# Feed-forward of an attention + top-4-block layer: from all tokens with a mask to 80 pages of gathered rows

## What is computed

```
x = x + attn(cond(x, itok_B_0_7, L0_cond_weights), Wq, bq, Wk, bk, Wv, bv, Wo)
x = x + ffn(cond2(x, itok_B_1_198, L0_cond2_weights), Wr, br, W1, W2)
```

```
prob = softmax(xf @ Wr.T + br)            # 2048 tokens, 16 blocks
_, idx = top_k(prob, 4)                   # each token keeps 4 blocks
h = einsum('nf,ibf->nib', xf, W1b)        # block i: 128 hidden units
h = gelu(h) * mask[:, :, None]            # exact gelu
y = einsum('nib,fib->nf', h, W2b)
```

## Time and profile before

| | |
|---|---|
| median of 3 runs | 896.96 us (895.66 to 899.36) |
| profiled execution, span | 899.2 us |
| what lies around the span in its own run | not given apart; the slowest of the three runs, 899.36 us, is 0.2 above the span |
| PE / DVE / ACT / POOL busy | 96% / 49% / 41% / 11% |
| chain that ended last | PE 72%, DVE 10%, ACT 6%, DMA 5%, issue 4% |
| DMA | 71.52 MB in 99,746 packets, mean 80 GB/s |
| granted TensorE clock | mean 0.992 |

### The profile page before, as it was taken

How to read it: one execution, slowest core, us unless ns; L and a number is a source line. 1 busy time by engine, 2 the same in 40 slices (tenths; PEclk the granted TensorE clock), 3 DMA queues, 4 the chain that set the end, 5 groups by cost and what they waited for, 6 DMA issues and landing times.

```text
span 899.2 us, 14422 instructions
## 1 busy us (share of the span) xinstructions
PE 866.4 (96%) x5250; PEld 430.9 (48%) x5250; DVE 439.4 (49%) x829; ACT 371.4 (41%) x639; POOL 100.9 (11%) x104
## 2 busy tenths in 40 slices
PE   6999999999899999999999999999999999999998
PEld 3444554445454445544445544454445444544443
DVE  3779773248762248752268766542254125403510
ACT  4678642147632157531267535530253025203400
POOL 3311111102111002220001100110011001100000
PEclk8999999999999999999999999999999999999999
DMA  7632432013441013330124598104210321031001
GB/s 220 226 129 61 84 70 71 12 62 56 90 82 36 13 61 85 75 76 23 59 74 96 114 262 274 26 2 142 73 26 12 141 61 26 23 129 36 0 24 47
DMA packets 99746, 71.52 MB, mean 80 GB/s; under 512 B 75828, under 2 KB 75892, under 8 KB 99700
## 3 DMA queue, kind: packets, MB, share of 16 engines
q10 hardware_dynamic: 75056, 34.71, 16.4%
q1 hardware_dynamic: 24644, 36.20, 12.6%
HBM read 45.66 MB, written 8.45 MB: 60 GB/s over the span
## 4 chain that ended last, share of the span: by engine, by line
PE 72%; DVE 10%; ACT 6%; DMA 5%; issue 4%; ACTq 2%; SPq 0%; POOL 0%; DVEq 0%
PE Q L935 57%; PE F L935 12%; DMA mids<-att 4%; PE M L935 3%; ACT u L437 2%; DVE sq L719 2%; ACTq L458 2%; ACT sq L443 2%; DVE att L740 1%; DVE att L732 1%; DVE e L714 1%; PE Q L1109 1%; DMA cw<-in_cw_dram 1%; DVE wa L890 1%; ACT e L436 1%
## 5 line engine op out<-in xcount | busy, mean ns | idle before, releaser
L935 PE MATMUL Q<-hT,wa 128*128 128x512 f16 x1536 | 342.7, 381 | 1.8 <-ACT e L591 1.8
L935 PEld LDWEIGHTS Q<-hT,wa 128*128 128x128 f16 x1536 | 148.6, 98 | 173.5 <-issue 2.8
L935 PE MATMUL Q<-wb,mids 128*128 128x512 f16 x768 | 175.5, 380 | 2.0 <-DVE xres L747 1.9
L935 PE MATMUL Q<-kv,mids 128*128 128x512 f16 x512 | 154.9, 379 | 0.0
L935 PEld LDWEIGHTS Q<-wb,mids 128*128 128x128 f16 x768 | 71.6, 98 | 83.9 <-DVE xres L747 2.0
L591 ACT ACTIVATE e<-Q,zero 128x512 f32<-128x512 f32 x64 | 43.9, 687 | 137.2 <-PE Q L935 137.2
L935 PE MATMUL Q<-sq,mids 128*128 128x512 f16 x256 | 97.0, 379 | 0.0
L343 POOL TENSOR_TENSOR xs<-xin,xs 128x512 f16<-128x512 f32 x32 | 39.7, 1239 | 503.0 <-ACT cws L396 503.0
L747 DVE SCALAR_TENSOR_TENSOR xres<-Q,xres 128x512 f32<-128x512 f32 x32 | 22.0, 689 | 127.5 <-PE Q L935 127.5
L935 PEld LDWEIGHTS Q<-kv,mids 128*128 128x128 f16 x512 | 50.1, 98 | 59.1
L714 DVE SCALAR_TENSOR_TENSOR e<-e,u 128x512 f32<-128x512 f32 x64 | 46.4, 725 | 54.8 <-ACT u L437 54.7
(11 more groups left out here) (97 smaller groups left out, 743.8 us busy)
## 6 DMA issues: line engine op xcount, KB each, us to landing
xin<-in_x_dram SPq DMA_DIRECT2D x16, 256.0 KB, 3.0
mids<-in_wq_dram SPq DMA_DIRECT2D x4, 1024.0 KB, 8.5
mids<-in_wo_dram SPq DMA_DIRECT2D x4, 1024.0 KB, 5.3
xres<-in_x_dram SPq DMA_DIRECT2D x16, 256.0 KB, 2.7
x_dram<-xres SPq DMA_DIRECT2D x16, 256.0 KB, 2.1
xin<-x_dram SPq DMA_DIRECT2D x16, 256.0 KB, 2.7
wk<-mask_dram ACTq DMA_DIRECT2D x8, 512.0 KB, 5.3
wv<-mask_dram ACTq DMA_DIRECT2D x8, 512.0 KB, 7.2
```

The source lines that it names most:

```text
L935: last = nc.tensor.matmul(out, lhs(a), rhs(b), start=(k == 0 and q == 0), stop=(k == n - 1 and q == len(PASSES) - 1))
```

## The change

The feed-forward no longer runs all blocks for all tokens. For each pair of batches m (16 in all, `NT`) the conditioned tokens are split into float16 high and low parts and routed as before (`cond2`, `router`, `route`). Then two small matmuls count: a strictly triangular and an all-ones matrix times the 0/1 mask give each token's position within its block and the number of tokens per block (`count`). `position` on DVE keeps for each of the 16 blocks a current page of 128 rows; when it is full the block takes the next free page. The result is a row number for each of a token's 4 kept blocks (`slot`). The two float16 parts of the tokens are turned back to rows of 2 KB by a transposing DMA (`turn_rows`, ACT), and POOL writes each row to its 4 places in a DRAM buffer of 80 pages (`scatter`, four indirect DMAs of 128 rows). The buffer is filled with zeros first (10 stores of 2 MB, issued by SP in group 0). A table gives each page's block (`table`).

After the attention SP loads each page with a transposing DMA (`load_slots`), PE applies the 128 hidden units of that page's block (12 matmuls of 128 columns, weights addressed by a register that is loaded from the table), four pages share a PSUM bank, ACT makes gelu, and the second layer is 3 matmuls of 512 columns per page; y rows are stored to DRAM (`store_slots`). When all are stored, POOL gathers for each pair of batches 4 x 128 rows of 2 KB, DVE adds them and x1, and SP stores the result. All loops are written out instead of looped. The routing of groups 0 and 1 is placed in the attention of groups 2 and 3's preparation (`routing`, in the code the bodies g = 1 and 2), that of groups 2 and 3 in `last_body`. Mask, mask broadcast and `body_b` are gone.

```diff
+NT = NG * NP
+NS = 80
+NQ = NS // 4
+ROWS = NS * 128
+NX, NC = 8, 6
+FILL = 10
...
+            def fill(i):
+                r = NS // FILL
+                sp.dma_start(xg_d.rearrange("(p r) c -> p r c", p=128)[:, r * i:r * i + r, :],
+                             rows[:, 0, :].unsqueeze(1).to_broadcast([128, r, 2 * T])).then_inc(filled, 16)
...
+            def load_slots(t):
+                if t == 0:
+                    sp.wait_ge(o_free, NP * NG + 1)
+                    for q in scat:
+                        sp.wait_ge(q, 64 * NT // 2)
+                elif t >= NX:
+                    sp.wait_ge(w1_done, (t - NX) // 4 + 1)
+                sp.dma_start_transpose(xT[:, t % NX, :, :], xg_d[128 * t:128 * t + 128, :]).then_inc(x_ld[t % NX], 16)
...
+            for t in range(NX):
+                load_slots(t)
+            for q in range(NQ):
+                for t in range(4 * q + NX, min(4 * q + NX + 4, NS)):
+                    load_slots(t)
+                for t in range(4 * q, 4 * q + 4):
+                    store_slots(t)
...
+            def scatter(m):
+                s = m % 2
+                pool.wait_ge(placed, m + 1)
+                pool.wait_ge(rows_in[s], 16 * (m // 2 + 1))
+                for k in range(TOPK):
+                    pool.indirect_dma_start(xg_d, bass.IndirectOffsetOnAxis(ap=slot[:, m, k:k + 1], axis=0),
+                                            rows[:, s, :], None).then_inc(scat[s], 16)
...
+                    kv_split(g + 1, 1)
+                    x_split(1, g - 1, 0)
+                    x_split(1, g - 1, 1)
+                    x_split(1, g - 1, 2)
+                    scatter(m)
+                    kv_split(g + 1, 2)
+                    x_split(1, g - 1, 3)
+                    scatter(m + 1)
+                    kv_split(g + 1, 3)
...
+            for j in range(4):
+                pool.wait_ge(y_st[j], 16 * NQ)
+            for m in range(NT):
+                c = m % NC
+                if m >= NC:
+                    pool.wait_ge(out_st[c], 16 * (m // NC))
+                for k in range(TOPK):
+                    pool.indirect_dma_start(cb[c][:, k, :], None, y_d,
+                                            bass.IndirectOffsetOnAxis(ap=slot[:, m, k:k + 1], axis=0)).then_inc(got[c], 16)
...
+            def first_layer(q):
+                s = q % 2
...
+                for j in range(4):
+                    t = 4 * q + j
+                    expert[t] = t if t < NB else pe.value_load(tab[0:1, t:t + 1], min_val=0, max_val=NB - 1)
+                    pe.wait_ge(x_ld[t % NX], 16 * (t // NX + 1))
+                    for k in range(KC):
+                        last = product(Q[s][:, j * 128:(j + 1) * 128], lambda a: wa[:, a, k, bass.ds(expert[t] * 128, 128)],
+                                       lambda b: xT[:, t % NX, 4 * b + k, :], k, KC)
+                last.then_inc(w1_done, 1)
...
+            for q in range(1, NQ):
+                first_layer(q)
+                second_layer(q - 1)
```

1275 lines of the change are left out of this document (838 added, 437 removed).

## The result

The changed kernel takes 942.52 us (median of 4 runs, 941.06 to 946.44), the kernel before on the same chip 896.31 (895.38 to 899.36): ratio 1.052, 95% interval 1.049 to 1.055. It is 5% slower. The prediction was 886 us with a range up to 938 and "faster" as its likeliest sign: wrong in value, range and sign.

The account below looks back on a forecast made before the run. The prediction took TensorE's matmul columns to bound the feed-forward half. Its terms, 624 us to the end of attention and routing, 7 hand-over, 170 pages and 87 gathers, gave 888 us, less 2: 886 us, range 846 to 938.

Parts of the forecast that it names:

- (a): Attention groups 0 to 2: routing adds 16 us, with a 4 us stall per group; the page fill in group 0 adds nothing.
- if that cover goes: Page fill in group 0: x loads and turned tiles would land late and PE wait; no size given.
- (b): Last attention group: DVE becomes the bound with 68 us against PE's 31, plus 6 us for the last two m.
- (c): Hand-over to the pages: last four scatters at 1.25 us, 5 us, and a landing 2.0; SP starts at 631.
- (d): Pages: transfers are the bound at 8.2 us per four pages, PE's sequencer at 6.5 hidden; 170 us in all.
- (e): Gather and sum at the end: 64 gathers at 1.25 us on POOL, DVE's 42 us of additions hidden; 87 us.
- Rival 2: Scatters and gathers bare on the path: POOL's issue at 2.0 us each costs 51 us more, 937 us; chance 0.20.
- Rival 3: Pages: TensorE's clock falls to 0.50, four pages take 10.2 us, 926 us in all; chance 0.08.
- Rival 4: Groups 1 and 2: routing chain stalls PE 14 us per group instead of 4, 906 us; chance 0.05.
- The sign: Whole kernel against the one before: faster 0.61, same 0.07, slower 0.32.

Follow-up runs that it names:

- fill_few: Against the changed kernel, only the 30 pages left partly empty are filled with zeros, in 5 stores of 1.5 MB; 931.55 us, ratio 1.036 to the kernel before.
- fill_fine2: Against the changed kernel, zero fill in 40 paced 0.5 MB pieces, group 0's x loads and stores moved ahead, 16 pieces at the end; 939.27 us.
- late: Against the changed kernel, last residual addition moved earlier, 32 of 46 PE fillers removed, fill paced in 33 pieces in group 0 and 7 in group 1; 929.05 us.
- no_position: Changed kernel without `position`: constant slots and one small DVE copy per m in its place, output not the reference's; 925.28 us.
- plain: Changed kernel with pages loaded plainly instead of turned, same bytes, output not the reference's; 930.2 us, ratio 1.035 to the kernel before.
- static: Changed kernel with constants for the pages' block numbers, so no value loads or register addresses on PE there; 939.5 us, ratio 1.045 to the kernel before.
- few_adds: Changed kernel with the three additions per m in the tail cut to one of 8 columns; 934.74 us, ratio 1.043 to the kernel before.
- warm: Changed kernel with two filler matmuls on PE ahead of the wait of each page from 8 on; 947.6 us, ratio 1.054 to the kernel before.
- no_scatter: Changed kernel without the 64 scatters, so the pages stay zero and the output is not the reference's; 923.45 us.
- half_gather: Changed kernel with each gather fetching half a row, 1 KB instead of 2, at the same number of instructions; 938.38 us, ratio 1.047 to the kernel before.

## Why the prediction was wrong

- **(a), "there is room for it, so nothing": failed, 15 us.** The fill was priced by its share of the engines over 160 us. What counts is who is behind a burst: two stores of 2 MB hold the 16 engines for some 10 us (396 GB/s), and the turned tiles that PE needs come behind them. fill_few, fill_fine2 and late show 12 to 14 of the 15. The sentence on what happens "if that cover goes" named the mechanism, and I gave it no chance.
- **(a), routing in groups 1 and 2: mechanism right, size off**, 23 us instead of 16. The stall was 7.7 us per group (11.7 of growth less PE's 4 us of new work) against my 4, and `position` costs 7.2 and 5.5 of it (no_position).
- **(b), the last group: failed, 10 us.** I added up DVE's 68 us and let "the order of PE" not matter. DVE was never full (66 us of work in 103), and taking 34 us of work from it gave 11. The chain goes from a late addition over store, x load, POOL's split behind scatters, and PE's fillers; 7 us of it came back by moving one addition and 32 fillers.
- **(c): right.** 4 x 1.27 us and a landing of 2.7 us, from the chain.
- **(d): failed, 11 us.** I put PE's sequencer at 6.5 us per four pages, "hidden as long as DMA is slower". It is not hidden: it needs 7.7 us at the least and 8.4 in plain, and in the changed kernel the pages lay ready before PE took them. The value load was priced too high (0.86 us; some 0.65 with its bookkeeping), but the eight address steps of a page take 1.0 us, not 0.3, and those of the second layer 1.1, not 0.5. The transfers took 8.4 (static), not 8.2. Beside each other the two make a step of 8.9, more than either.
- **(e): the issue price was right, the cover failed, 9 us.** An undisturbed issue takes 1.255 us against my 1.25; I had no row for it and took the turning transfer's, so that it fits is luck. The tail was still 9 us longer: 7.5 of it the additions beside the gathers (few_adds). "DVE's 42 us of additions ... are hidden" failed.
- Rival 2 (POOL's issue at over 1.4) did not come, but nearly: the mean was 1.375, with the additions' part in it, and its remark that DVE adds beside POOL was right. Rival 3 did not either, though the clock did fall to 0.88: held at 1.00 it gave nothing (warm). Rival 4 is between: the stall of 7.7 us per group lies between my 4 and its 14, and it came from `position` on DVE, as in (a), not from the scatters ahead of `kv_split` (no_scatter: 1.8 and 0.6 us).
- The sign: no single rival brought it. Five terms were each short by 7 to 15 us in the same direction, and the range knew only one case going wrong at a time.

## What to carry over

A transfer priced by its share of an idle DMA is not free: ask which small transfer on the critical path will stand behind its burst, pace it, and see what the pacing queue itself then holds up. Count what a register address costs the sequencer: here eight address steps and a value load took 1.65 us for 12 matmuls that the array does in 0.83, and a bound that was put down as hidden set the pace. Two resources with the same total per step, 8.4 us each, took 8.9 together. A plan made of many covered terms (five here) errs to one side; give that case a chance of its own.

## What the runs showed that I had not expected

- An indirect transfer of 128 rows costs POOL 0.95 us and 0.30 to the next one, whether its rows have 1 or 2 KB (medians of 946 and 1,068 ns for the two groups of gathers with 2 KB, 954 and 949 in half_gather); the durations after, ns min/median/max:

```profile
L560 POOL DMA_INDIRECT wb<-y_dram,slot x36: 942/946/1994, 844.5 to 925.9; - x36
L507 POOL DMA_INDIRECT xg_dram<-rows,slot x64: 954/960/1633, 309.7 to 660.5; - x64
L430 SPq DMA_TRANSPOSE mids<-xg_dram x80: 1286/1307/2848, 663.3 to 828.4; - x80
```

- A DVE step of 16 columns can be shut out for 3.98 us when POOL goes from a scatter straight into three subtractions, and yet the group loses little by it (no_scatter).
- Twelve matmuls of 128 columns with register addresses take 1.11 us, and 0.15 to 0.72 us of issue before them, where the array has caught up with the sequencer; where the sequencer is ahead they take 0.83, as with constants (0.84).
- In late, the pages took 6 us longer than in the changed kernel, with the same code there. PE's sequencer waited 6.5 us longer for pages; why they came later stays open.
